# In every group VectorE adds the last quarter of the slots onto the third quarter, and TensorE's identity matmuls sum six of eight slots

## The chip, the cores and the metric

The kernel runs on one core of a Trainium2 chip. The metric is the device time of one execution in microseconds. TensorE (PE in the profile), VectorE (DVE), ScalarE (ACT), GpSimd (POOL) and SyncE (SP) are the five engines of the core. Each works through its own list of instructions in order, and they meet only at semaphores.

## What is computed

The reference is two layers over a graph of 6250 nodes and 200,000 edges, with 16 features each; the edges are sorted by their target node `dst`.

```python
w_m = (efeat @ W_msg + b_msg).reshape(E, in_f, -1)      # 16 x 16 per edge
w_a = (efeat @ W_attn + b_attn).reshape(E, in_f, -1)
h_src = feat[src][:, :, None]
e1 = w_m * h_src
e2 = w_a * h_src
ex = jnp.exp(e2 - seg_max[dst])
denom = segment_sum(ex, dst)
ft = segment_sum(e1 * (ex / denom[dst]), dst).sum(axis=1)
x = layernorm(x + ft)
x = layernorm(x + segment_mean(edge_attr, dst))
```

So each edge has 512 numbers of its own (256 of `e2`, 256 of `e1`), made from its 16 attributes and from the 16 features of its source node. For each node the sums over its edges of `ex` and of `e1 * ex` are wanted. 200,000 edges of 512 numbers are what the time goes into.

## The kernel before

Nodes are sorted by degree and put into 49 tiles (`NC`) of 128 nodes, one node per partition. Tile k has `DEG[k]` slots, from 56 down to 22: slot j holds the j-th edge of each of its 128 nodes. All 49 tiles have 1630 slots, of which 1607 need features. A tile's slots are cut into groups of 8 or 6 (`sizes`, `GRP`): 152 groups of 8 and 69 groups of 6, 221 in all.

For each slot, in order:

- GpSimd gathers the features of the 128 source nodes, with one indirect DMA per slot (`gather`, L647 to L653), into `HGF`, a ring of 80 slots (`FR`). Per tile it also loads the edge records (`edges_of`, L657), and for 36 tiles it scatters a result (L694). The index of each indirect DMA is a column in SBUF.
- TensorE transposes the edge attributes (`T`, L1097), ScalarE copies them out of PSUM (`evac`, L888), and TensorE makes the 512 weights of the slot (`W`, L1108) in one of two pairs of PSUM banks.
- VectorE multiplies two slots' weights with the gathered features into `EMR`, a ring of 64 slots (`mult`, L1472, a custom instruction that takes the maximum along). Before a tile's first multiplication `floors` (L1458) waits until the gathers of the tile have landed; only in the first and the last tile it waits group by group.
- Once a tile is complete its maximum is known. ScalarE takes the exponential of the first half of the group into PSUM (L944), then of the whole group in place (L946), then copies the second half's (L950) into PSUM. VectorE multiplies each half with its exponentials (`gm`, L1485).
- TensorE sums the slots of the group: one fp32 matmul with the identity per slot, all accumulated in the PSUM tile `PDR` (`gsum`, L1111 to L1131). After the last group of a tile ScalarE copies `PDR` out (L894) and VectorE divides and reduces (`weigh`, L1504 to L1506).

The order is written out by hand as `STEPS` (L106 to L118), 236 steps. In step i group p is produced (T, W, `mult`) and group c is consumed (exponentials, `gm`); TensorE sums the group that was consumed in step i-1. In TensorE's list the parts are interleaved (L1143 to L1149): up to four pairs of W, and behind each of them a quarter of the sums, that is 2 slots; T of group p+2 comes after the second quarter. On VectorE a step is two `mult`, `gm` of the first half, two `mult`, `gm` of the second half, and then what a new tile needs (L1600 to L1635).

For the last four groups alone (`ADDS`, L145) there is one operation more: `pairs` (L1487 to L1493) adds, in SBUF, the last slots of the second half onto the slots before them, and `gsum` leaves those last slots out. `KEPT(half)` is how many slots of the second half are kept: 2 of 4 in a group of 8, and 2 of 3 in a group of 6.

```python
def pairs(g):
    half = GRP[g][2] // 2
    keep = KEPT(half)
    v.wait_ge(S["a_exp"], g + 1)
    v.wait_ge(S["v_gm"], 2 * g + 2)
    sums = em(g, half, 2 * half - keep)
    v.tensor_tensor(sums, sums, em(g, half + keep, 2 * half), ALU.add).then_inc(S["v_ad"], 1)
```

Of the kernel before, what the change touches and what calls it, by code (L numbers as in the profile page):

```python
# [94 lines left out]
for g in range(NGR):  # L95
    n = GRP[g][2]
# [9 lines left out]
STEPS, MADE, USED, p, c = [], {}, {}, 0, 0  # L106
# [17 lines left out]
for g in range(NGR):  # L124
    k, n = GRP[g][0], GRP[g][2]
# [16 lines left out]
FINS = {USED[LAST[k]]: k for k in range(NC)}  # L142
NST = len(STEPS) + 4
NORMS = [p for p, c in STEPS].index(FIRST[MAIN + 4] + 2)
ADDS = [c for p, c in STEPS[-8:] if p is None]  # L145


def KEPT(n):
    return (n + 1) // 2


def gnn_kernel(nc, xt, dst, src, ea, eat, es, wc, cst, cst2, out):
# [14 lines left out]
    with ctx:  # L167
# [3 lines left out]
        def sem(name):  # L171
            return ctx.enter_context(nc.semaphore(name))
# [226 lines left out]
        S = {n: sem(n) for n in names}  # L399
# [42 lines left out]
        def em(g, lo=0, hi=None):  # L442
            hi = GRP[g][2] if hi is None else hi
            return EMR[:, 512 * (AT[g] + lo):512 * (AT[g] + hi)]
# [10 lines left out]
        def part(k, lo, hi):  # L455
            return XP[:, roff[k % 2]:roff[k % 2] + DEG[k], lo:hi]
# [588 lines left out]
        def _(pe):  # L1045
# [38 lines left out]
            def regular():  # L1084
                pe.wait_ge(S["v_xm"], 2)
                pe.wait_ge(S["g_m"], 9)
                pe.wait_ge(S["d_w2"], 160)
                pe.wait_ge(S["v_id"], 1)

                def T(g):  # L1090
                    k, j0, n, a = GRP[g]
                    pe.wait_ge(S["v_x3"], k + 1)
                    pe.wait_ge(S["a_p"], 4 * k + 4)
                    if g >= 1:
                        pe.wait_ge(S["a_T"], g)
                    for j in range(n):
                        i = pe.transpose(PTB[0:K, 128 * j:128 * j + 128], part(k, 0, K)[:, j0 + j, :], IDB[:, :])  # L1097
                    i.then_inc(S["p_T"], 1)

                def W(g, x):  # L1100
                    s = FROM[g] + x
                    if x == 0:
                        pe.wait_ge(S["a_T"], g + 1)
                    if s >= 2:
                        pe.wait_ge(S["v_mult"], s - 1)
                    for j in range(2):
                        lo = 128 * (PAIR[s][1] + j)
                        i = pe.matmul(PAIRS[s % 2][:, j, :], LT[:, g % 3, lo:lo + 128], WS[:, :], start=True, stop=True)  # L1108
                    i.then_inc(S["p_W"], 1)

                def gsum(g, lo, hi):  # L1111
                    k, j0, n, a = GRP[g]
                    half = n // 2
                    if g in ADDS:
                        n = half + KEPT(half)
                    for j in range(lo, min(hi, n)):
                        if j == 0:
                            if a == 0 and k >= 1:
                                pe.wait_ge(S["a_dn"], k)
                            pe.wait_ge(S["a_exp"], g + 1)  # L1120
                            pe.wait_ge(S["v_gm"], 2 * g + 1)
                        if j == half:
                            if g in ADDS:
                                pe.wait_ge(S["v_ad"], ADDS.index(g) + 1)
                            else:
                                pe.wait_ge(S["v_gm"], 2 * g + 2)
                        x = em(g, j, j + 1).rearrange("p (i a o) -> p a i o", a=2, o=16)
                        i = pe.matmul(PDR, IDN, x, start=(a == 0 and j == 0),  # L1128
                                      stop=(g == LAST[k] and j == n - 1))
                        if j == n - 1:  # L1130
                            i.then_inc(S["p_g"], 1)  # L1131

                T(0)
                T(1)
                W(0, 0)
                W(0, 1)
                for i in range(NST):
                    p, c = STEPS[i] if i < len(STEPS) else (None, None)
                    nx = STEPS[i + 1][0] if i + 1 < len(STEPS) else None
                    old = STEPS[i - 1][1] if 1 <= i <= len(STEPS) else None  # L1140
                    ahead = [(p, x) for x in range(2, GRP[p][2] // 2)] if p is not None else []
                    ahead += [(nx, 0), (nx, 1)] if nx is not None else []
                    for x in range(4):  # L1143
                        if x < len(ahead):
                            W(*ahead[x])
                        if old is not None:
                            gsum(old, 2 * x, 2 * x + 2)
                        if x == 1 and p is not None and p + 2 < NGR:
                            T(p + 2)  # L1149

# [109 lines left out]
        def _(v):  # L1260
# [154 lines left out]
            def regular():  # L1415
# [21 lines left out]
                def diff(k):  # L1437
                    v.wait_ge(S["v_ev"], k + 1)
                    if k >= 1:
                        v.wait_ge(S["a_p"], 4 * k)  # L1440
                    v.tensor_tensor(RM[:, 0:DEG[k], :], edge(k), upper(edge(k)), ALU.subtract).then_inc(S["v_x1"], 1)
# [19 lines left out]
                def mult(s):  # L1461
                    g, j = PAIR[s]
                    k = GRP[g][0]
                    if j == 0:
                        v.wait_ge(S["v_hm"], HMS[g])
                        if OLD[g] is not None:
                            v.wait_ge(S["p_g"], OLD[g] + 1)
                    v.wait_ge(S["p_W"], s + 1)
                    w = PAIRS[s % 2].rearrange("p j (i c) -> p (j i) c", c=32)
                    hb = feat(g, j, j + 2).unsqueeze(2).broadcast_to([128, 32, 32])  # L1470
                    x = s - FROM[FIRST[k]]
                    v.tensor_tensor_reduce(em(g, j, j + 2).rearrange("p (x c) -> p x c", c=32), w, hb, 1.0, LOW, ALU.mult, ALU.max,  # L1472
                                           accum_out=MXC[:, k % 2, x:x + 1]).then_inc(S["v_mult"], 1)
# [13 lines left out]
# [7 lines that stand above are left out]
# [102 lines left out]
                for i in range(NST):  # L1596
                    p, c = STEPS[i] if i < len(STEPS) else (None, None)
                    nx = STEPS[i + 1][0] if i + 1 < len(STEPS) else None
                    ahead = [FROM[p] + x for x in range(GRP[p][2] // 2)] if p is not None else []
                    for s in ahead[0:2]:  # L1600
                        mult(s)
                    if c is not None:
                        gm(c, 0)
                    for s in ahead[2:4]:
                        mult(s)
                    if p is not None and p == LAST[GRP[p][0]]:
                        collapse(GRP[p][0])
                    if c is not None:
                        gm(c, 1)
                        if c in ADDS:  # L1610
                            pairs(c)
                    if nx is not None:
                        k = GRP[nx][0]
                        if k in (0, NC - 1):
                            floors(nx, nx + 1)
                        elif nx == FIRST[k]:
                            for seg in SEGS:
                                if GRP[seg[0]][0] == k:
                                    floors(seg[0], seg[-1] + 1)
                    if p is not None:  # L1620
                        for k in range(1, NC):
                            if p == max(FIRST[k] - 6, 0):
                                valid(k)
                            if p == FIRST[k] - 5:
                                diff(k)
                            if p == FIRST[k] - 4:
                                low(k)
                            if p == FIRST[k] - 3:
                                mean(k)
                    if i - 3 in FINS:  # L1630
                        weigh(FINS[i - 3])
                        if FINS[i - 3] >= NC - 2:
                            joined(FINS[i - 3])
                    if 0 <= i - NORMS < 14:
                        main(i - NORMS)  # L1635
# [358 lines left out]
```

## Time and profile before

| | us |
|---|---|
| median of 3 runs without the profiler | 2243.48 (2243.09 to 2245.55) |
| span of the profiled execution, first to last instruction | 2950.2 |
| PE busy (matmuls) | 2137.9, 72% |
| DVE busy | 1862.0, 63% |
| POOL busy | 1687.5, 57% |
| ACT busy | 1256.9, 43% |
| granted TensorE clock, mean | 0.861 |

The profiled execution took 706.7 us longer than the median of the runs, so shares of its span can't be read as shares of 2243. Durations of single instructions can be read, and so can the time that one engine waited for another. PE is the busiest engine by the page.

### The profile page before, as it was taken

Reading aid. Unit: us, or ns where it says so; the run is one execution under the profiler, and the core shown is the slowest. Engines: PE = TensorE matmul, PEld = TensorE weight load, DVE = VectorE, ACT = ScalarE, POOL = GpSimd, SP = SyncE. Lnnn points to the kernel's source line nnn. Section 1 sums busy time; section 2 is a strip of 40 time slices with the busy share of each in tenths; the row PEclk is TensorE's granted clock in tenths of the full one; section 3 lists DMA queues with packets and bytes.
Section 4 is the critical chain, followed back from the end, with each engine's and each line's share of the span. In section 5 each row is a group of like instructions: output and inputs, shape, how many; then the busy total and the mean of one; then the engine's idle time right before and its main releaser. Section 6 shows DMA issues by size and latency. Waiting matters only on the chain. (4 is left out here: it accounts for less than half of the span.)

```text
span 2950.2 us, 21765 instructions
## 1 busy us (share of the span) xinstructions
PE 2137.9 (72%) x6682; PEld 952.6 (32%) x6682; DVE 1862.0 (63%) x2907; ACT 1256.9 (43%) x1228; POOL 1687.5 (57%) x1845
## 2 busy tenths in 40 slices
PE   2347676676877777877787658877787767887777
PEld 1213233232333333333333223333333323333333
DVE  6246465566666666666676547766667656786776
ACT  3223443434444443454454325444444444554444
POOL 6556355665655565555565465655656565655633
PEclk8658888897988888989888889988989888988988
DMA  6000000000000000000000000000000001001000
GB/s 229 16 10 11 8 12 10 10 10 9 10 9 9 14 10 9 10 14 10 10 13 9 9 10 13 10 12 9 10 12 9 12 9 28 12 8 16 8 2 3
DMA packets 60073, 47.60 MB, mean 16 GB/s; under 512 B 28366, under 2 KB 55439, under 8 KB 59436
## 3 DMA queue, kind: packets, MB, share of 16 engines
q0 software_dynamic: 57632, 29.73, 8.0%
q1 hardware_dynamic: 2316, 16.38, 1.5%
q8 instruction: 57, 0.93, 0.1%
q14 instruction: 68, 0.56, 0.1%
HBM read 44.00 MB, written 1.90 MB: 16 GB/s over the span
## 5 line engine op out<-in xcount | busy, mean ns | idle before, releaser
L652 POOL DMA_INDIRECT AR<-in_xt,AR x1607 | 1538.8, 958 | 974.1 <-DVE AR L1472 491.3
L1128 PE MATMUL PX<-AR,CS 128*128 128x512 f32 x3246 | 1663.7, 642 | 37.8 <-issue 23.9
L1472 DVE CUSTOM_DVE_ANT_1 AR<-PW,AR 128x1024 f32<-128x1024 f32 x815 | 979.6, 1221 | 896.8 <-remote 651.2
L1108 PE MATMUL PW<-WS,LT 100*128 100x512 bf16 x1630 | 549.1, 423 | 683.9 <-DVE AR L1472 511.8
L1128 PEld LDWEIGHTS PX<-AR,CS 128*128 128x128 f32 x3246 | 664.9, 206 | 652.1 <-issue 532.4
L888 ACT ACTIVATE LT<-PTB 100x1024 bf16<-100x1024 bf16 (+1 forms) x221 | 211.2, 956 | 1005.7 <-remote 601.0
L1485 DVE TENSOR_TENSOR AR<-AR,PX 128x1024 f32<-128x1024 f32 (+1 forms) x442 | 501.0, 1134 | 121.3 <-ACT PX L944 76.0
L1108 PEld LDWEIGHTS PW<-WS,LT 100*128 100x128 bf16 x1630 | 141.5, 103 | 1113.7 <-DVE AR L1472 543.2
L946 ACT ACTIVATE AR<-AR 128x2048 f32<-128x2048 f32 (+1 forms) x221 | 412.9, 1869 | 7.2
L950 ACT ACTIVATE PX<-AR 128x1024 f32<-128x1024 f32 (+1 forms) x221 | 212.4, 961 | 412.3 <-DVE AR L1485 294.8
L944 ACT ACTIVATE PX<-AR 128x1024 f32<-128x1024 f32 (+1 forms) x221 | 231.0, 1045 | 39.4 <-DVE AR L1485 30.1
L1097 PEld LDWEIGHTS PTB<-IDB,AR 128*100 128x100 bf16 x1630 | 133.4, 135 | 139.0 <-issue 138.2
L1097 PE MATMUL PTB<-IDB,AR 128*100 128x128 bf16 x1630 | 138.4, 231 | 10.3 <-ACT AR L922 9.1
L657 POOL DMA_INDIRECT AR<-in_es,E0I x48 | 47.1, 982 | 169.5 <-DVE AR L1472 143.4
L894 ACT ACTIVATE AR<-PX 128x512 f32<-128x512 f32 x49 | 29.2, 597 | 144.7 <-PE PX L1128 66.1
L1504 DVE RECIPROCAL AR<-AR 128x256 f32<-128x256 f32 x49 | 85.5, 1746 | 1.9 <-ACT AR L894 1.9
L1472 DVE DVE_READ_ACCUMULATOR2_ANT AR<- 128x1 f32 x815 | 67.6, 83 | 0.0
L914 ACT ACTIVATE AR<-AR 128x1024 bf16<-128x1024 bf16 (+13 forms) x49 | 54.8, 1119 | 0.0
L922 ACT ACTIVATE AR<-AR 128x1024 bf16<-128x1024 bf16 (+13 forms) x49 | 54.1, 1105 | 0.0
L1497 DVE TENSOR_REDUCE AR<-AR 128x16 f32<-128x512 f32 (+13 forms) x49 | 52.3, 1067 | 0.0
L694 POOL DMA_INDIRECT y_d<-AR x36 | 36.0, 1000 | 11.0 <-issue 11.0
L1458 DVE TENSOR_TENSOR AR<-AR 128x128 f32<-128x128 f32 (+14 forms) x71 | 36.7, 536 | 0.9 <-issue 0.2
(192 smaller groups left out, 517.7 us busy)
## 6 DMA issues: line engine op xcount, KB each, us to landing
AR<-in_xt,AR POOLq DMA_INDIRECT x1607
AR<-in_eat SPq DMA_DIRECT2D x3, 3128.0 KB
AR<-in_eat SPq DMA_DIRECT2D x1, 3120.0 KB
y_d<-AR SPq DMA_DIRECT2D x1, 784.0 KB
AR<-y_d SPq DMA_DIRECT2D x1, 784.0 KB
AR<-in_es,E0I POOLq DMA_INDIRECT x48
y_d<-AR POOLq DMA_INDIRECT x36
CS<-in_cst SPq DMA_DIRECT2D x1, 442.0 KB, 5.3
```

The source lines that it names most:

```text
L652: g.indirect_dma_start(feat(h, j - j0, j - j0 + 1), None, xt, bass.IndirectOffsetOnAxis(ap=node, axis=0)).then_inc(hg_sem(h), 16)
L888: a.activation(LT[:, g % 3, 0:128 * n], PTB[0:K, 0:128 * n], ACT.Copy).then_inc(S["a_T"], 1)
L914: a.activation(part(k, 0, 96).rearrange("p j (x w) -> p j x w", x=2)[:, :, :, 0:16], twice(h), ACT.Copy)\
L944: a.activation(half(w), x[:, 0:w, :], ACT.Exp, bias=shift).then_inc(S["a_x"], 1)
L946: a.activation(x, x, ACT.Exp, bias=shift).then_inc(S["a_exp"], 1)
L950: a.activation(half(w), x[:, w:2 * w, :], ACT.Copy).then_inc(S["a_x"], 1)
L1097: i = pe.transpose(PTB[0:K, 128 * j:128 * j + 128], part(k, 0, K)[:, j0 + j, :], IDB[:, :])
L1108: i = pe.matmul(PAIRS[s % 2][:, j, :], LT[:, g % 3, lo:lo + 128], WS[:, :], start=True, stop=True)
L1128: i = pe.matmul(PDR, IDN, x, start=(a == 0 and j == 0), stop=(g == LAST[k] and j == n - 1))
L1472: v.tensor_tensor_reduce(em(g, j, j + 2).rearrange("p (x c) -> p x c", c=32), w, hb, 1.0, LOW, ALU.mult, ALU.max, accum_out=MXC[:, k % 2, ...
L1485: v.tensor_tensor(y, y, EXP[:, 0:16 * w].rearrange("p (x o) -> p x o", o=16), ALU.mult).then_inc(S["v_gm"], 1)
L1504: link(v.reciprocal(RRT, d[:, 0:256]))
```

## The change

Every group is now treated as the last four were. `ADDS` is gone. VectorE calls `pairs` for each group right behind its second `gm`. `gsum` always sums `half + KEPT(half)` slots, 6 of 8 or 5 of 6, and its second half waits for the addition (`v_ad`) and no longer for `gm`. The sums behind the four pairs of W are no longer 2, 2, 2, 2 but 1, 2, 1, 2 slots (`GSUM`).

```diff
-ADDS = [c for p, c in STEPS[-8:] if p is None]
+
+
+GSUM = [(0, 1), (1, 3), (3, 4), (4, 6)]
...
                     half = n // 2
-                    if g in ADDS:
-                        n = half + KEPT(half)
+                    n = half + KEPT(half)
...
                         if j == half:
-                            if g in ADDS:
-                                pe.wait_ge(S["v_ad"], ADDS.index(g) + 1)
-                            else:
-                                pe.wait_ge(S["v_gm"], 2 * g + 2)
+                            pe.wait_ge(S["v_ad"], g + 1)
...
                         if old is not None:
-                            gsum(old, 2 * x, 2 * x + 2)
+                            gsum(old, *GSUM[x])
...
                     if c is not None:
                         gm(c, 1)
-                        if c in ADDS:
-                            pairs(c)
+                        pairs(c)
```

## Rows read from the trace of the kernel before

**Rows 1.** Groups by line and form: busy us, mean ns of one, idle before it

```profile
L1128 PE MATMUL PX<-AR,CS 128*128 128x512 f32 x3246 | 1663.7, 642 | 37.8 <-issue 23.9 <-ACT AR L894 13.8
L652 POOL DMA_INDIRECT AR<-in_xt,AR x1607 | 1538.8, 958 | 974.1 <-DVE AR L1472 491.3 <-issue 478.7 <-DMA AR<-in_es,E0I 3.1
L1472 DVE CUSTOM_DVE_ANT_1 AR<-PW,AR 128x1024 f32<-128x1024 f32 x815 | 979.6, 1221 | 896.8 <-remote 651.2 <-PE PW L1108 145.7 <-issue 83.4
...
L657 POOL DMA_INDIRECT AR<-in_es,E0I x48 | 47.1, 982 | 169.5 <-DVE AR L1472 143.4 <-DVE E0I L1398 18.1 <-issue 8.1
```

**Rows 2.** TensorE in order of time: start us, us, line, how many

```profile
107.33 1.06 PE L1097 MATMUL PTB<-IDB,AR 128*100 128x128 bf16 x8 [9.10 <-ACT AR L922]
...
2863.38 0.60 PE L1108 MATMUL PW<-WS,LT 100*128 100x512 bf16 x2
2863.81 1.88 PE L1128 MATMUL PX<-AR,CS 128*128 128x512 f32 x4
2865.53 0.61 PE L1097 MATMUL PTB<-IDB,AR 128*100 128x128 bf16 x8
2865.98 0.60 PE L1108 MATMUL PW<-WS,LT 100*128 100x512 bf16 x2
```

**Rows 3.** GpSimd in order of time: the start of tile 1, and the last gather

```profile
91.58 0.94 POOL L657 DMA_INDIRECT AR<-in_es,E0I  x1 [18.13 <-DVE E0I L1398]
95.64 0.94 POOL L652 DMA_INDIRECT AR<-in_xt,AR  x1 [3.12 <-DMA AR<-in_es,E0I]
96.89 0.94 POOL L652 DMA_INDIRECT AR<-in_xt,AR  x1 [0.30 <-issue]
...
2800.94 0.94 POOL L652 DMA_INDIRECT AR<-in_xt,AR  x1 [0.30 <-issue]
```

**Rows 4.** VectorE in order of time: the last `mult`, and additions of the last groups

```profile
2898.59 1.22 DVE L1472 CUSTOM_DVE_ANT_1 AR<-PW,AR 128x1024 f32<-128x1024 f32 x1
...
2906.11 1.22 DVE L1485 TENSOR_TENSOR AR<-AR,PX 128x1024 f32<-128x1024 f32 x1 [1.87 <-ACT PX L950]
2907.43 1.23 DVE L1493 TENSOR_TENSOR AR<-AR 128x1024 f32<-128x1024 f32 x1
2908.58 1.75 DVE L1504 RECIPROCAL AR<-AR 128x256 f32<-128x256 f32 x1
...
2926.15 0.69 DVE L1493 TENSOR_TENSOR AR<-AR 128x512 f32<-128x512 f32 x1
2926.76 1.74 DVE L1504 RECIPROCAL AR<-AR 128x256 f32<-128x256 f32 x1
```

**Rows 5.** VectorE and GpSimd: gathers that start inside an operation with two SBUF inputs

```profile
526.02 1.08 DVE L1448 TENSOR_TENSOR AR<-AR 128x896 bf16<-128x896 f32 x1
526.18 1.74 POOL L652 DMA_INDIRECT AR<-in_xt,AR  x1 [0.30 <-issue]
...
1777.95 0.69 DVE L1441 TENSOR_TENSOR AR<-AR 128x512 f32<-128x512 f32 x1
1778.03 1.42 POOL L652 DMA_INDIRECT AR<-in_xt,AR  x1 [0.30 <-issue]
```

**Rows 6.** The same where the VectorE operation reads one input from PSUM

```profile
1540.61 1.22 DVE L1472 CUSTOM_DVE_ANT_1 AR<-PW,AR 128x1024 f32<-128x1024 f32 x1
1541.14 0.94 POOL L652 DMA_INDIRECT AR<-in_xt,AR  x1 [0.30 <-issue]
1541.75 1.22 DVE L1485 TENSOR_TENSOR AR<-AR,PX 128x1024 f32<-128x1024 f32 x1
```

**Rows 7.** Single lines with two SBUF inputs: duration ns min/median/max (L1441), busy and mean (L1458)

```profile
L1441 DVE TENSOR_TENSOR AR<-AR x49: 517/690/1087, 104.0 to 2838.0; 128x512 f32<-128x512 f32 x7, 128x480 f32<-128x480 f32 x7, 128x544 f32<-128x544 f32 x6, 128x608 f32<-128x608 f32 x5
...
L1458 DVE TENSOR_TENSOR AR<-AR 128x128 f32<-128x128 f32 (+14 forms) x71 | 36.7, 536 | 0.9 <-issue 0.2
```

**Rows 8.** Two stretches: busy us of PE, PEld, DVE, ACT, POOL; granted clock

```profile
1498.00:1526.00 28.00, 27.65 (x93) 12.69 (x92) 23.16 (x34) 13.75 (x15) 14.24 (x16) 1.00 0.06 5
1538.00:1549.00 11.00, 7.92 (x19) 2.98 (x20) 10.17 (x16) 9.31 (x9) 8.26 (x10) 0.53 0.17 31
```

## The prediction

> **What bounds the kernel now.** I read the page first, then the groups by form, then each engine in order of time. By the page PE is the bound: 2137.9 us busy. But the profiled execution is 706.7 us longer than the median without the profiler, 2243.48, and the first thing to settle is where these went. 651.2 us of them are VectorE's: it stands before `mult` with a releaser that the trace does not name ("remote"), in 123 stalls [rows 1]. 2950.2 - 651.2 = 2299, near the median; I take these stalls to belong to the profiled execution. So I use its durations and ask what each engine would need without them.
>
> TensorE: in a stretch without stalls it is busy for 27.65 of 28 us at granted clock 1.00, its full level of 2.4 GHz [rows 8]. There a pair of W takes 0.43 us, four sum matmuls (two slots) 1.72 us, eight transposes 0.45 us [rows 2]. The 3246 sum matmuls [rows 1] are two for each of 1623 slots: 3246 x 0.43 = 1396 us. W is 815 x 0.43 = 350 us, the transposes 1630 / 8 x 0.45 = 92 us. Sum 1838 us. It begins at 107.3 [rows 2], and the end without work of its own is some 20 us: 1965 us, 278 less than measured.
>
> GpSimd: gathers follow each other every 1.25 us (95.64, 96.89), 0.94 us and 0.30 of issue, wherever it does not wait [rows 3]. Its idle time behind VectorE is 491.3 + 143.4 = 634.7 us [rows 1], nearly the stalls' 651.2: it waits for free slots of the ring only because VectorE stands. The last gather starts at 2800.9 [rows 3]; without those waits at 2166.2. To that: landing, 4.1 us by the edge record (issued at 91.58, its reader starts at 95.64) [rows 3]; `floors` and three `mult` of the last group, 3.7; and from the end of the last `mult` at 2899.8 [rows 4] to the end of the span, 50.4. Sum 2224 us, 19 below the median.
>
> So the GpSimd list of some 1690 indirect DMAs is the bound, not PE. It is a floor that the change doesn't lower: tile k can't start until its gathers have landed, and the next tile's are issued meanwhile. A tile of 38 slots costs GpSimd 38 x 1.25 and 2.5 for the record and the result, 50 us; TensorE 38 x (0.86 + 0.215 + 0.056) = 43 us.
>
> **What the change removes.** 149 groups of 8 and 68 of 6 are new in it (152 and 69 less the last four). TensorE loses 2 x 149 + 68 = 366 slots, 732 matmuls x 0.43 = 315 us. All of it lies beside GpSimd's list: worth nothing at the end. In the tail nothing goes either, the last four groups had it already. TensorE's total falls to 1523 us.
>
> **What it adds.** 217 operations on VectorE, just the form of L1493. One of 128x1024 starts 1.32 us after the `gm` before it and not 1.14, as it waits for that one's result, and the next operation follows 1.15 us later: 1.33 us in all. That of 128x512 is 0.61 + 0.18 = 0.79 [rows 4, 6]. 149 x 1.33 + 68 x 0.79 = 252 us. Does VectorE become the bound? Its list today: `mult` 815 x 1.15 = 937; `gm` 304 x 1.14 + 138 x 0.86 = 465; the page's other busy time 1862.0 - 979.6 - 67.6 (its accumulator reads) - 501.1 = 314. Sum 1716, then 1968; from 107 to its end some 2095 us, below GpSimd's 2224. Per tile of 38 slots: 40 us now, 46 then, against 50. So I cost this at nothing, but the cover is down to a tenth; if it were gone, each per cent more on VectorE's list would be 20 us.
>
> **The waits.** `pairs` waits for the group's exponentials, which the `gm` before it already had. Queued behind it are `floors`, the preparation of tiles and the next two `mult`; TensorE's W waits for those, with two pairs of PSUM banks between. TensorE's new wait for `v_ad` concerns the group of the step before, and stands behind a W that needs a later `mult`: never last. The split 1, 2, 1, 2 moves no W by more than 0.86 us; I cost it at zero, with GpSimd's list as the cover. DMAs are neither added nor moved in any queue.
>
> **What it costs GpSimd.** The addition has both inputs in SBUF, and there are four lines of this kind in each tile now (L1434, L1441, L1448, L1458). When a gather starts inside one, it is held. At 526.18 it starts 0.16 us into L1448 and takes 1.74 us, not 0.94; at 1778.03 it starts 0.08 into L1441 and takes 1.42 [rows 5]. Held time is in both the rest of the operation less 0.12 or 0.13 us. A gather that starts inside a `mult`, one input of which is in PSUM, takes 0.94 [rows 6]. So an addition of 1.23 us holds a gather by at most 1.10 us, one of 0.69 by 0.565. With a gather every 1.25 us at a phase that is not tied to VectorE's, the mean is 1.10² / 2.5 = 0.484 us, and 0.128. Sum: 149 x 0.484 + 68 x 0.128 = 81 us, all of it on the list that bounds. Bounds from both sides: no gather ever meets an addition, 0; each meets one at its start, 149 x 1.10 + 68 x 0.565 = 202. Check of the mean on today's lines: 147 of 0.69 us and 71 of 0.54 [rows 7] should hold by 147 x 0.128 + 71 x 0.07 = 24 us if GpSimd never waited; the gathers' mean of 958 against the usual 942 ns is 1607 x 0.016 = 26 us [rows 1]. So the mean is not too high, perhaps low. I take 85.
>
> The Trainium skill has both readings on one page, "SBUF — State Buffer", section "Who interferes with whom". It says that a VectorE instruction with two SBUF inputs contends with a GpSimd instruction that reads SBUF, and an indirect DMA reads its index column there; but it also infers that making descriptors needs only the write side, so that `tensor_tensor` does not stall such DMAs. By the second the time would stay at 2243. The trace agrees with the first: 0.80 us held.
>
> **Sum.** 2243.5 + 85 = 2328 us (+3.8%). Against the profiled execution's own sum: 2224 + 85 = 2309 and the 19 us that my floor lacks. Own range of this case: 2285 to 2350.
>
> **Rivals.**
> 1. Faster. The 1.25 us per gather may be a price of the profiler; without it GpSimd would be quicker and PE the bound of today. For it: PE is back to back in clean stretches [rows 8], and 1838 / 0.861, the profiled mean clock, + 127 = 2262 is near the median too. Against it: the half level (0.53) comes where PE has been idle [rows 8], and a PE that bounds has no such idle time. Then VectorE's 2095 plus some 50 of waits at 49 tile starts decides: 2145. It decides once GpSimd's floor and the 85 together are under 2243, that is at a real pace below 1.25 x (2158 - 154) / (2224 - 154) = 1.21 us (154 is what of the floor is not pace: 95.6 ahead and 58 behind).
> 2. No change. GpSimd bounds, but gathers and additions don't meet: the additions come at a fixed place of a step and might fall in step with the gathers, or GpSimd has slack that the profile hides. 2243. Against: rows 5.
> 3. Much slower. PE now has work for 1523 of 2330 us, 65%, in many short pieces, and may be granted the 1.2 GHz level more often. It decides once the mean clock is under 1523 / 2200 = 0.69; at 0.65 it is 1523 / 0.65 + 127 = 2470. In the stretch at 0.53 PE was busy for 7.92 of 11 us [rows 8]; but stretches as poor as that followed stalls.
>
> **Chances.** Forecast 0.66, rival 1 0.14, rival 2 0.10, rival 3 0.07, others 0.03. The range from 2240 to 2365 takes in rival 2 and more than the forecast's own range; outside are rival 1 and most of rival 3. A measurement of this kernel can tell about 0.2%, 4.5 us, from no change. Rival 2 goes mostly into "same", rival 1 and a bit of it into "faster": faster 0.16, same 0.08, slower 0.76.
>
> **What would show it.** In the profile after: 2514 sum matmuls; L1493 x221; L652's mean well above 958 ns, by 85 / 1.6 = 53 ns if GpSimd never waited, less as far as it waits; gathers of up to 2.0 us that start within L1493 and none within `mult`; GpSimd's idle time behind VectorE no smaller than its stalls make it. I am wrong on the bound if the time falls below 2230, wrong on the hold if L652 keeps its mean, and wrong on the clock if the granted mean without stalls is under 0.7.

## The result, and the profile after

| | before | after |
|---|---|---|
| median of the runs made together, us | 2243.28 (2241.71 to 2245.55, 4 runs) | 2310.03 (2307.34 to 2312.91, 4 runs) |
| ratio, 95% interval | 1 | 1.0296 (1.0282 to 1.0311) |

The change makes the kernel 66.8 us slower. The forecast was 2328, its range 2240 to 2365.

The profiled execution of the changed kernel took 2307.9 us, as long as its unprofiled runs; the stalls of 651.2 us [rows 1] are not in it. First the page's busy times, then the groups by line (busy us, mean ns of one, idle before it and what ended it). Numbers of lines have moved by two: L652 is now L654, L657 is L659, L1128 is L1126, L1472 is L1470, L1458 is L1456, L1493 is L1491.

```profile
span 2307.9 us, 20735 instructions
## 1 busy us (share of the span) xinstructions
PE 1762.1 (76%) x5950; PEld 792.0 (34%) x5950; DVE 2067.3 (90%) x3124; ACT 1257.8 (54%) x1228; POOL 1738.0 (75%) x1845
```

```profile
L654 POOL DMA_INDIRECT AR<-in_xt,AR x1607 | 1587.0, 988 | 493.2 <-issue 485.1 <-DVE AR L1470 3.7 <-DMA AR<-in_es,E0I 3.0
L1126 PE MATMUL PX<-AR,CS 128*128 128x512 f32 x2514 | 1311.3, 637 | 4.7 <-ACT AR L896 4.7
L1470 DVE CUSTOM_DVE_ANT_1 AR<-PW,AR 128x1024 f32<-128x1024 f32 x815 | 967.4, 1219 | 27.4 <-PE PW L1110 17.8 <-PE PX L1126 4.9 <-issue 3.1
L1110 PE MATMUL PW<-WS,LT 100*128 100x512 bf16 x1630 | 549.7, 423 | 464.0 <-DVE AR L1470 462.6
...
L1491 DVE TENSOR_TENSOR AR<-AR 128x1024 f32<-128x1024 f32 x152 | 186.5, 1227 | 16.2 <-DVE AR L1483 0.5
...
L1491 DVE TENSOR_TENSOR AR<-AR 128x512 f32<-128x512 f32 x69 | 47.9, 694 | 7.2
```

What was to be removed is gone: 2514 sum matmuls and not 3246. TensorE now stands 462.6 us before W, waiting for VectorE. What was added is there: 221 additions, 234.4 us. The gathers' idle time is nearly all small pieces of 0.3 us of issue, one before each; GpSimd waits for VectorE for 3.7 us in the whole run. So nothing holds it back, and still its 1607 gathers take 988 ns each. Compared with [rows 1], where it is 958, that is 48 us of longer gathers.

Where these are, two stretches of the timeline show (start us, us, engine and line; in brackets the idle time before).

```profile
316.57 0.94 POOL L654 DMA_INDIRECT AR<-in_xt,AR  x1 [0.30 <-issue]
...
317.76 1.23 DVE L1491 TENSOR_TENSOR AR<-AR 128x1024 f32<-128x1024 f32 x1
317.82 1.98 POOL L654 DMA_INDIRECT AR<-in_xt,AR  x1 [0.30 <-issue]
...
1519.55 1.23 DVE L1491 TENSOR_TENSOR AR<-AR 128x1024 f32<-128x1024 f32 x1
...
1520.34 1.26 POOL L654 DMA_INDIRECT AR<-in_xt,AR  x1 [0.30 <-issue]
```

The first gather starts 0.06 us into the addition and takes 1.98 us, 1.04 more than its 0.94. The second starts 0.79 us into one and takes 0.32 more. Both come to 1.10 or 1.11 us after the addition's start: a gather that starts within a 1.23 us addition is held until 0.12 us before the addition's end. That is the law the prediction read from two older lines [rows 5]. Added up over all indirect DMAs that start in L1491 (gathers, and a few of the edge records and scatters), the time over 942 ns is 60.4 us, in 148 of them.

The law has an exception at its very start. Of 157 indirect DMAs that start in an addition at least 0.13 us before its end, 152 obey it within 0.05 us. The other five start within 0.044 us of the addition's own start and are not held at all; there the addition takes longer. One of them:

```profile
410.79 1.28 DVE L1491 TENSOR_TENSOR AR<-AR 128x1024 f32<-128x1024 f32 x1
410.81 0.94 POOL L654 DMA_INDIRECT AR<-in_xt,AR  x1 [0.30 <-issue]
```

The three long additions among these five take 1.26 to 1.30 us, not 1.23.

### The profile page after: what moved, and what is told of

Its sections match the earlier page's. It is cut to its first block and busy times, and to the rows that moved or that the text cites. A ratio compares the mean times of both kernels' runs of the same rounds, so it can differ in the third digit from the quotient of the medians.

```text
span 2307.9 us, 20735 instructions
## 1 busy us (share of the span) xinstructions
PE 1762.1 (76%) x5950; PEld 792.0 (34%) x5950; DVE 2067.3 (90%) x3124; ACT 1257.8 (54%) x1228; POOL 1738.0 (75%) x1845
## 5 line engine op out<-in xcount | busy, mean ns | idle before, releaser
L654 POOL DMA_INDIRECT AR<-in_xt,AR x1607 | 1587.0, 988 | 493.2 <-issue 485.1
L1126 PE MATMUL PX<-AR,CS 128*128 128x512 f32 x2514 | 1311.3, 637 | 4.7 <-ACT AR L896 4.7
L1470 DVE CUSTOM_DVE_ANT_1 AR<-PW,AR 128x1024 f32<-128x1024 f32 x815 | 967.4, 1219 | 27.4 <-PE PW L1110 17.8
L1110 PE MATMUL PW<-WS,LT 100*128 100x512 bf16 x1630 | 549.7, 423 | 464.0 <-DVE AR L1470 462.6
L1126 PEld LDWEIGHTS PX<-AR,CS 128*128 128x128 f32 x2514 | 517.5, 206 | 407.3 <-issue 292.6
L1483 DVE TENSOR_TENSOR AR<-AR,PX 128x1024 f32<-128x1024 f32 (+1 forms) x442 | 500.8, 1133 | 45.8 <-ACT PX L946 23.2
L1491 DVE TENSOR_TENSOR AR<-AR 128x1024 f32<-128x1024 f32 (+1 forms) x221 | 234.4, 1061 | 23.4 <-DVE AR L1483 0.5
L1099 PEld LDWEIGHTS PTB<-IDB,AR 128*100 128x100 bf16 x1630 | 126.2, 129 | 131.7 <-issue 129.8
L1099 PE MATMUL PTB<-IDB,AR 128*100 128x128 bf16 x1630 | 131.5, 224 | 10.3 <-ACT AR L924 9.0
L1456 DVE TENSOR_TENSOR AR<-AR 128x128 f32<-128x128 f32 (+14 forms) x71 | 37.2, 543 | 93.0 <-DMA AR<-in_xt,AR 92.4
L1470 DVE DVE_READ_ACCUMULATOR2_ANT AR<- 128x1 f32 x815 | 67.4, 83 | 0.0
L896 ACT ACTIVATE AR<-PX 128x512 f32<-128x512 f32 x49 | 29.2, 596 | 58.7 <-PE PX L1126 58.5
L659 POOL DMA_INDIRECT AR<-in_es,E0I x48 | 46.7, 974 | 14.6 <-issue 13.1
```

Source lines behind the costliest of these rows:

```text
L654: g.indirect_dma_start(feat(h, j - j0, j - j0 + 1), None, xt, bass.IndirectOffsetOnAxis(ap=node, axis=0)).then_inc(hg_sem(h), 16)
L1126: i = pe.matmul(PDR, IDN, x, start=(a == 0 and j == 0), stop=(g == LAST[k] and j == n - 1))
L1483: v.tensor_tensor(y, y, EXP[:, 0:16 * w].rearrange("p (x o) -> p x o", o=16), ALU.mult).then_inc(S["v_gm"], 1)
```

## The experiments

**The kernel before once more.** No edit.

> The kernel before, profiled once more, to see whether its 651 us of stalls with an unnamed releaser belong to the kernel or to that one profiled execution. Theory (GpSimd's list of indirect DMAs bounds, the stalls belong to the profiled execution): time 2243; if this execution has fewer stalls, GpSimd runs on from tile 1 to the last gather with next to no wait for VectorE, the gathers' mean rises from 958 to some 960 to 965 ns (more of them meet the existing operations with two SBUF inputs), and PE is idle for 15 to 20% of the span. Rival (PE bounds the kernel before): PE has next to no idle time between its start and the end, and GpSimd waits for free slots for 100 us or more.

The 651.2 us of stalls did not come back: the profiled execution took 2243.2 us. TensorE is busy for 1963.1 us of it, so idle for 12% and not for the 15 to 20% expected, and the gathers' mean is 956 ns, a little under the 960 to 965; GpSimd's gathers wait for VectorE for 7.3 us, where the rival asked for 100. This is the trace with which the others are compared. Its rows: the gathers, `mult`, and in order of time the last gather, the 721st `mult` and the last `mult`.

```profile
L652 POOL DMA_INDIRECT AR<-in_xt,AR x1607 | 1536.1, 956 | 493.1 <-issue 481.1 <-DVE AR L1472 7.3 <-DMA AR<-in_es,E0I 3.1
L1472 DVE CUSTOM_DVE_ANT_1 AR<-PW,AR 128x1024 f32<-128x1024 f32 x815 | 974.8, 1220 | 162.9 <-PE PW L1108 113.5 <-issue 24.8 <-PE PX L1128 22.5
...
2162.24 0.94 POOL L652 DMA_INDIRECT AR<-in_xt,AR  x1 [0.30 <-issue]
...
1955.93 1.22 DVE L1472 CUSTOM_DVE_ANT_1 AR<-PW,AR 128x1024 f32<-128x1024 f32 x1
...
2191.59 1.22 DVE L1472 CUSTOM_DVE_ANT_1 AR<-PW,AR 128x1024 f32<-128x1024 f32 x1
```

The same three in the changed kernel:

```profile
2214.25 0.94 POOL L654 DMA_INDIRECT AR<-in_xt,AR  x1 [0.30 <-issue]
...
2002.67 1.22 DVE L1470 CUSTOM_DVE_ANT_1 AR<-PW,AR 128x1024 f32<-128x1024 f32 x1
...
2256.15 1.22 DVE L1470 CUSTOM_DVE_ANT_1 AR<-PW,AR 128x1024 f32<-128x1024 f32 x1
```

So the last gather starts 52.0 us later; the gathers and the other indirect DMAs of this stretch are held for 77.5 us after and 26.4 before, and the difference, 51.1, accounts for nearly all of that delay. The 721st `mult` is 46.7 us later, the last one 64.6. What follows the last `mult` is the same (51.6 and 51.8 us from its start). The question for the other runs: are the 47 to 52 us the held gathers, and what are the 18 us between the 721st `mult` and the last?

**The addition with one input.**

```diff
-                    v.tensor_tensor(sums, sums, em(g, half + keep, 2 * half), ALU.add).then_inc(S["v_ad"], 1)
+                    v.tensor_reduce(ADR[:, 0:1], em(g, half + keep, 2 * half), AX.X, ALU.max).then_inc(S["v_ad"], 1)
```

> The changed kernel, with the added operation replaced by a reduction (maximum) over the same 1024 or 512 numbers: one SBUF input in place of two, about the same time on VectorE. The fourth quarter's slots are then left out of the sums. Theory (the addition costs because it holds gathers): the time goes back to 2243 to 2255 and the gathers' mean to 958 to 965 ns. Rival (VectorE's list, 252 us longer, has become the bound or trails GpSimd at the end): the time stays at 2300 to 2312. In between, about 2275, if each has half.

2260.06 us (2259.3 to 2260.67), ratio 1.0069 (1.0052 to 1.0086). VectorE does as much as in the changed kernel (2062.5 us busy, 2067.3 there), and 50 of the 67 us are gone. The gathers' group, and one of them that starts 0.10 us into the reduction:

```profile
L655 POOL DMA_INDIRECT AR<-in_xt,AR x1607 | 1535.0, 955 | 493.2 <-issue 478.8 <-DVE AR L1471 10.4 <-DMA AR<-in_es,E0I 3.1
...
1422.51 1.22 DVE L1492 TENSOR_REDUCE ADR<-AR 128x1 f32<-128x1024 f32 x1
1422.61 0.94 POOL L655 DMA_INDIRECT AR<-in_xt,AR  x1 [0.30 <-issue]
...
2160.44 0.94 POOL L655 DMA_INDIRECT AR<-in_xt,AR  x1 [0.30 <-issue]
...
2206.51 1.22 DVE L1471 CUSTOM_DVE_ANT_1 AR<-PW,AR 128x1024 f32<-128x1024 f32 x1
```

134 indirect DMAs start at least 0.13 us before the end of a long reduction and take 944 ns in the mean; in the changed kernel 124 start so in a long addition and take 1381. The last gather is as early as before (2160.4), the last `mult` is not (2206.5, 14.9 late). So the hold doesn't come from VectorE being busy or from its reading as such. The reduction also writes one number per partition and not 1024, but writing isn't the cause either: in the changed kernel 264 indirect DMAs start as early within the long `gm` (L1483), which writes 1024 numbers to SBUF and reads one input from PSUM, and they take 945 ns in the mean. What is left is the second input in SBUF. At 2260 the time is above the 2243 to 2255 of my expectation: a second loss, some 15 us, is VectorE's own.

This run also shows how the indirect DMAs' starts lie against the added operation when nothing is held. Had the law held for them, they would have been held for 83 us, which is what the prediction took.

**The addition alone, all slots still summed.**

```diff
-GSUM = [(0, 1), (1, 3), (3, 4), (4, 6)]
+GSUM = [(0, 2), (2, 4), (4, 6), (6, 8)]
...
-                    n = half + KEPT(half)
```

> The changed kernel, but TensorE sums all 8 (or 6) slots again, 2, 2, 2, 2 behind the four W; the additions stay, so the fourth quarter is counted twice. Theory (TensorE's relief is worth nothing, it lies beside GpSimd's list): 2305 to 2320, as the change. Rival (TensorE is close to the bound, and the relief hides part of the additions' price): 2243 + 250 or so, 2400 to 2500.

2316.99 us (2314.2 to 2320.08), ratio 1.0323 (1.0305 to 1.034). The indirect DMAs are held for 73.8 us and the last gather starts at 2209.8. TensorE's 732 matmuls bring the changed kernel 7 us at most; and as the pieces of the sums differ too, the run further down has to say which of the two brings them.

**The relief alone: six of eight slots summed, no addition.**

```diff
+GSUM = [(0, 1), (1, 3), (3, 4), (4, 6)]
...
-                    if g in ADDS:
-                        n = half + KEPT(half)
+                    n = half + KEPT(half)
...
-                            gsum(old, 2 * x, 2 * x + 2)
+                            gsum(old, *GSUM[x])
```

> The kernel before, but TensorE sums only 6 of 8 and 5 of 6 slots in every group and VectorE adds nothing (but in the last four groups, as before); the slots left out are not counted. This is the change's relief alone, 315 us of TensorE. Theory (GpSimd's list bounds): 2235 to 2245, no change. Rival (TensorE bounds the kernel before): 1960 to 2150.

2249.05 us (2246.14 to 2250.28), ratio 1.0016 (1.0006 to 1.0026). TensorE's busy time falls from 1963.1 to 1741.9 us and no time is gained by it; the kernel is, if anything, 0.2% slower. `floors` shows where it went: it waits for gathers 37 times and 211.0 us, where it waited 21 times and 96.8 in the kernel before.

```profile
L1460 DVE TENSOR_TENSOR AR<-AR x71: 244/583/1091, 89.0 to 2187.2; 128x128 f32<-128x128 f32 x11, 128x480 f32<-128x480 f32 x9, 128x256 f32<-128x256 f32 x7, 128x512 f32<-128x512 f32 x6
its engine sat idle before it (us, times) until:
  DMA AR<-in_xt,AR: 211.0, 37
```

**The addition in two and in four pieces.** The same numbers are added, by two or by four instructions.

```diff
-                    v.tensor_tensor(sums, sums, em(g, half + keep, 2 * half), ALU.add).then_inc(S["v_ad"], 1)
+                    w = 512 * (half - keep) // 4
+                    more = em(g, half + keep, 2 * half)
+                    for x in range(4):
+                        i = v.tensor_tensor(sums[:, w * x:w * x + w], sums[:, w * x:w * x + w], more[:, w * x:w * x + w], ALU.add)
+                    i.then_inc(S["v_ad"], 1)
```

> The changed kernel, each addition cut into two of half the size, with the same result. Theory (a gather that starts inside an operation with two SBUF inputs is held for the rest of that operation less 0.125 us): held time of an addition goes with the square of its length. Two pieces of 0.69 us hold 2 x 0.565 x 0.565 / 2.5 = 0.26 us where one of 1.23 held 0.48; of the 51 us that the additions put on GpSimd's list some 25 stay. VectorE's list grows by 217 x 0.07 = 15 us. Time 2285 to 2295. Rival (the additions take bandwidth or slots from GpSimd in proportion to what they move): list and time as in the change, 2310, or 2315 to 2325 with the further instructions.

> The changed kernel, each addition cut into four. Theory: four pieces of about 0.35 us hold 4 x 0.225 x 0.225 / 2.5 = 0.08 us; of the 51 us some 8 stay on GpSimd's list. VectorE's list grows by some 40 us against the change, and it trails GpSimd further at the end: the 15 us of the kernel with one input become 20 to 40. Time 2265 to 2295. Rival (in proportion to the data): 2310 or more, up to 2350.

In two: 2293.94 us (2293.67 to 2296.58), ratio 1.0228 (1.0213 to 1.0244). In four: 2290.5 us (2289.09 to 2294.89), ratio 1.0214 (1.0198 to 1.0229). One line of each, by source line (duration ns min/median/max):

```profile
L654 POOL DMA_INDIRECT AR<-in_xt,AR x1607: 940/944/1687, 25.7 to 2195.6; - x179
```

```profile
L654 POOL DMA_INDIRECT AR<-in_xt,AR x1607: 940/945/1592, 24.9 to 2189.7; - x179
```

Worked out from the traces, all in us:

| | held in the addition | held in all | last gather starts | from there to the end |
|---|---|---|---|---|
| before | 0 | 26.4 | 2162.2 | 81.0 |
| one piece | 60.4 | 77.5 | 2214.3 | 93.7 |
| two pieces | 37.5 | 58.5 | 2195.6 | 96.3 |
| four pieces | 23.0 | 53.8 | 2189.7 | 98.9 |

A gather is held by the piece that it meets, not by the next one too, so shorter pieces hold it for less. Both times lie in their expected ranges, but less was saved than expected: I had expected some 25 and 8 us to stay of the change's 51, and 37.5 and 23.0 are held in the additions. In four, this is the length that I took for a piece, 0.35 us; the pieces of 128x256 take 0.42, and with that the expectation's own formula gives 23. What is held in the additions falls from 60.4 to 23.0, in all only from 77.5 to 53.8: the operations directly behind the addition hold more gathers again. One that has been held by the addition goes on just before its end and has gone before the next operation could catch it; this shielding is worth some 9 us in one piece (17.1 us held outside the addition, 26.4 in all before) and is gone in four (30.8). `low` (L1448 before, L1446 after), which follows directly behind the addition in 45 of 49 cases, shows it: it holds for 5.1 us in the kernel before, 1.0 behind one piece and 6.4 behind four.

**The scatters left out of the kernel before.** It asks whether GpSimd's list sets the time also without a profiler.

```diff
-                    g.indirect_dma_start(YD, bass.IndirectOffsetOnAxis(ap=NODE[:, k:k + 1], axis=0), OUTR[:, k, :], None)\
-                     .then_inc(S["d_y"], 16)
+                    if k == MAIN - 1:
+                        g.indirect_dma_start(YD, bass.IndirectOffsetOnAxis(ap=NODE[:, k:k + 1], axis=0), OUTR[:, k, :], None)\
+                         .then_inc(S["d_y"], 16)
```

> The kernel before, with 1 in place of 36 of the scatters of results on GpSimd's list (L694); the output lacks the other 35 tiles' results. Nothing else changes on any engine. Theory (GpSimd's list bounds the kernel before, and its 36 scatters cost 1.29 us each as any other entry of it): 2243 - 35 x 1.29 = 2198, at most 10 us more if VectorE then trails. Rival (TensorE or VectorE bounds): 2238 to 2245.

2199.85 us (2196.78 to 2201.58), ratio 0.9803 (0.9788 to 0.9818), with 35 indirect DMAs fewer: 43.5 us by the medians, 1.24 us for each. TensorE's and VectorE's work is untouched. The pace of 1.25 us [rows 3] is that of unprofiled runs, and it is what bounds.

**The old operations of the kernel before in pieces.** Lines L1434, L1441, L1448 and L1458 in three pieces, then in two. One of the four:

```diff
-                    v.tensor_tensor(RM[:, 0:DEG[k], :], edge(k), upper(edge(k)), ALU.subtract).then_inc(S["v_x1"], 1)
+                    for lo, hi in cut(DEG[k]):
+                        e = edge(k)[:, lo:hi, :]
+                        i = v.tensor_tensor(RM[:, lo:hi, :], e, upper(edge(k))[:, lo:hi, :], ALU.subtract)
+                    i.then_inc(S["v_x1"], 1)
```

> The kernel before without the change, but its four operations with two SBUF inputs per tile (L1434, L1441, L1448, L1458) are each cut into three along the slots, with the same result. Theory: what they hold on GpSimd's list, 26 us, falls to a third or less: three pieces of 0.28 us hold 3 x 0.155 x 0.155 / 2.5 = 0.03 us where one of 0.69 held 0.13. 18 to 22 us come off the list, VectorE's grows by 400 x 0.06 = 24 us, which has room. Time 2222 to 2232, faster than both kernels. Rival (held time goes with the data, or VectorE's growth counts): 2243 to 2260.

> The kernel before, with VectorE's long SBUF-to-SBUF operations on two inputs (those of lines L1434, L1441, L1448 and L1458) each cut in two pieces instead of the three of the run e8_before_pieces; nothing else differs and all is computed. Theory (a gather that starts within such an operation is held until the operation's end less 0.12 us, and what is saved is only that held time, against more instructions on VectorE): held time over 942 ns of the gathers' DMAs 18 to 22 us where the kernel before has 26, so 2236 to 2240 us, within 0.1% of the version in three. Rival (the gain of that version came from another thing, such as the order in which VectorE's pieces release work): in two pieces the time is that of the kernel before, 2243 us, or under 2232.

In three: 2236.96 us (2235.2 to 2238.89), ratio 0.997 (0.996 to 0.9981). In two: 2235.08 us (2233.24 to 2235.64), ratio 0.9963 (0.9948 to 0.9977). Held time falls from 26.4 to 18.0 and 15.6 us, the last gather starts at 2154.2 and 2151.5. Both beat the kernel before and the changed one; the intervals don't tell the two apart. The first gained less than its expectation (2222 to 2232): I had put all of the 26 us to these four lines, and in the kernel before only 17.2 are held in them. They fall to 9.7 in three pieces and to 7.7 in two. The second came out just below what was expected, in its time (2236 to 2240) and in its held time (18 to 22).

```profile
L653 POOL DMA_INDIRECT AR<-in_xt,AR x1607 | 1526.9, 950 | 493.3 <-issue 481.2 <-DVE AR L1485 7.3 <-DMA AR<-in_es,E0I 3.2
```

**The sums in even pieces.** The changed kernel, with the pieces behind the four pairs of W cut as before the change.

```diff
-GSUM = [(0, 1), (1, 3), (3, 4), (4, 6)]
+GSUM = [(0, 2), (2, 4), (4, 6), (6, 8)]
```

> The changed kernel with one edit: the list by which a group's plane weights are summed and multiplied on is cut 2, 2, 2, 2 of the slots instead of as in the changed kernel, so that VectorE's products and TensorE's sums come in even pieces. The addition is untouched. Theory (what is lost is gathers held within the addition, and VectorE ending late behind the last gather): nothing changes, 2308 to 2313 us, held time over 942 ns of the gathers' DMAs 73 to 82 us. Rival (the order in which a group's pieces come ready sets when the addition starts against the gathers): an edit of this place moves the additions' starts and with them the held time by more than 10 us, so under 2300 or over 2322 us.

2326.94 us (2323.46 to 2329.04), ratio 1.0367 (1.0351 to 1.0384): 17 us worse than the changed kernel. Neither side of the expectation is right. My theory said that nothing changes; the rival has the time, over 2322, but for a cause, more held time, which is the wrong one, since it fell from 77.5 to 69.6 us and the last gather starts at 2205.8, 8.4 us earlier. The loss is behind it: 121.1 us from there to the end, 93.7 in the changed kernel. VectorE waits for W:

```profile
L1470 DVE CUSTOM_DVE_ANT_1 AR<-PW,AR 128x1024 f32<-128x1024 f32 x815 | 969.8, 1218 | 93.4 <-PE PW L1110 89.3 <-PE PX L1126 2.8 <-issue 0.3
...
2276.90 1.22 DVE L1470 CUSTOM_DVE_ANT_1 AR<-PW,AR 128x1024 f32<-128x1024 f32 x1
```

89.3 us, where it is 17.8 in the changed kernel. And it no longer waits for gathers. The line of `floors` from 440 us to the end, in this kernel and then in the changed one:

```profile
L1456 DVE TENSOR_TENSOR AR<-AR x57: 250/586/785, 495.4 to 2273.2; 128x480 f32<-128x480 f32 x8, 128x128 f32<-128x128 f32 x7, 128x512 f32<-128x512 f32 x6, 128x256 f32<-128x256 f32 x6
its engine sat idle before it (us, times) until:
who waited for it (us, times):
```

```profile
L1456 DVE TENSOR_TENSOR AR<-AR x57: 251/586/798, 495.6 to 2250.5; 128x480 f32<-128x480 f32 x8, 128x128 f32<-128x128 f32 x7, 128x512 f32<-128x512 f32 x6, 128x256 f32<-128x256 f32 x6
its engine sat idle before it (us, times) until:
  DMA AR<-in_xt,AR: 50.9, 22
```

In the changed kernel VectorE meets GpSimd 22 times in this stretch and for the last time at 1949 us; with even pieces never after 440. There VectorE's list with its waits is the bound for most of the run. The kernel with the full sums is the same case: it has even pieces too, and `floors` waits for gathers 3 times in it, for 21.1 us. Compared with that one (2316.99), fewer matmuls with even pieces bring nothing (2326.94), so the 7 us of the changed kernel are not TensorE's relief by itself; the pieces 1, 2, 1, 2 are worth 17. Why even pieces with fewer sums are 10 us slower than even pieces with all of them isn't settled; the two differ in how long TensorE works behind the third and the fourth pair, and I did not follow it further.

**The addition not in the late groups, and in them alone.** In groups 185 to 216 of 221, which the changed kernel consumes from about 1966 us on.

```diff
+ADDS = [g for g in range(NGR) if g < 185 or g >= NGR - 4]
...
-                    n = half + KEPT(half)
+                    if g in ADDS:
+                        n = half + KEPT(half)
...
-                            gsum(old, *GSUM[x])
+                            gsum(old, *(GSUM[x] if old in ADDS else (2 * x, 2 * x + 2)))
...
-                        pairs(c)
+                        if c in ADDS:
+                            pairs(c)
```

> The changed kernel without the addition in groups 185 to 216 of 221 (14 of 8 slots, 18 of 6; they are consumed from about 1966 us on); there TensorE sums all slots again, 2 behind each pair of W. The last four groups keep theirs, as in the kernel before. All is computed. Theory (until about 1950 us VectorE is held to the gathers' pace and the loss is held gathers; from there to the end VectorE sets the time, and each late addition is paid at its full length): the late additions' held time, 6.5 us, and what the changed kernel loses behind that point, 13 to 18 us, are gone, and all before it stays: 2286 to 2294 us. Rival (the whole loss is held gathers): only the 6.5 us come back, 2303 us.

> The mirror image: the kernel before, with the addition from group 185 on only (32 groups more than before; TensorE sums 6 of 8 slots there, in pieces of 1, 2, 1, 2). All is computed. Theory (from about 1950 us on VectorE sets the end): +13 to +20 us on the kernel before, 2256 to 2263 us, nearly all of it behind the last gather, whose start moves by 5 to 8 us only. Rival (the whole loss is held gathers): 6.5 us, 2250 us.

Beside these two the kernel before took 2247.59 us, 4 more than beside the changed kernel. Not late: 2293.35 us (2286.76 to 2297.01), ratio 1.0197 (1.0181 to 1.0212), so 22 us back by the two ratios (0.0099 x 2243) and 17 by the medians; the theory, 6.5 us and 13 to 18, asked for 20 to 24. Late only (the second has `g >= 185`): 2265.34 us (2260.36 to 2268.17), ratio 1.0067 (1.0052 to 1.0081), 15 to 18 us lost, a median 2 us above the expected 2256 to 2263. The 721st and the last `mult` of each:

```profile
1997.62 1.22 DVE L1475 CUSTOM_DVE_ANT_1 AR<-PW,AR 128x1024 f32<-128x1024 f32 x1
...
2230.93 1.22 DVE L1475 CUSTOM_DVE_ANT_1 AR<-PW,AR 128x1024 f32<-128x1024 f32 x1
```

```profile
1962.36 1.22 DVE L1475 CUSTOM_DVE_ANT_1 AR<-PW,AR 128x1024 f32<-128x1024 f32 x1
...
2214.82 1.22 DVE L1475 CUSTOM_DVE_ANT_1 AR<-PW,AR 128x1024 f32<-128x1024 f32 x1
```

Between them lie 233.3 and 252.5 us; before it was 235.7, after 253.5. So the last stretch takes 17 to 20 us longer exactly where the late additions are, whatever comes earlier. 27 of the 32 late additions lie in it, four before the 721st `mult` and one behind the last. The rival (2303 and 2250) is out. One thing of the theory is not as expected: in the kernel with late additions alone the last gather starts at 2176.2, 13.9 us later than before, and not 5 to 8. Of that, 5.5 us are there by the 701st `mult` (1910.9 against 1905.4), and the first of the added additions starts at 1925.5 only: this much two executions differ by themselves. The other 8.4 are about what was expected.

## Why the prediction came out

**What bounds: right.** GpSimd's list is the bound before. TensorE alone relieved brings nothing, 35 indirect DMAs fewer bring 1.24 us each without a profiler, and the last gather, put at 2166.2 when the waits are taken out, starts at 2162.2 in the undisturbed trace. Taking the 651.2 us for that execution's own was right: no later profile has them. What my floor of 2224 lacked, 19 us, lies behind the last gather: 58 us by my sum, 81.0 in the trace. I had let VectorE follow the last gather by one group; its last `mult` starts 29.4 us after it. That was the trace of the second term of the loss, and I passed over it. TensorE was closer to the bound than my 1838 us of work at full clock: it was busy for 1963.1 at a mean granted clock of 0.951.

**What it removes: right, worth nothing.** 732 matmuls fewer; alone, 1.0016.

**What it costs GpSimd: the right mechanism, the term mis-sized.** I took 85 us, from a mean of 0.484 us for each long addition. Measured are 60.4 us in the additions, and 51.1 net of the shielding of the operations behind them, which I had not thought of. The law of a single hold was right (152 of 157 within 0.05 us); the phase was wrong. I took the gathers' starts as spread evenly. The number that meet a long addition is what that gives: of the 144 long ones in the stretch of gathers 20 meet none, 17 by an even spread. But the starts within them are not even. By tenths of a us from the addition's start:

```
0.0  0.1  0.2  0.3  0.4  0.5  0.6  0.7  0.8  0.9  1.0
  8    5    6    7   12    8   18   19    9   17   15
```

Nearly two thirds lie in the later half, where little is left to be held for. "Not tied to VectorE's phase" was the step that failed, and the holds themselves tie it. In the kernel with one input, where nothing is held, the law put on the starts as they are gives 83 us; put on the changed kernel's it gives 64. How a hold moves the next starts is argued, not shown: a held gather goes on at a time that the addition's end sets, and the next ones follow 1.25 us apart.

Of the 34 us between 85 and 51, 4 are my rounding up of 81, some 2 are five additions behind the last gather, 15 the phase, 3 the few that start with the addition and are not held, and 9 the shielding. The old lines should have warned me. The same mean gives 24 us for them, and I set the 26 us of the gathers' longer mean beside it, but in the undisturbed trace only 17.2 of its 26.4 are held in the four lines, where 15 of 76 indirect DMAs that start in one of them begin within 0.042 us of its start and are not held. The rest is other lines and a few ns on each gather. So the mean was too high, not "perhaps low".

**What it adds to VectorE: costed at nothing, cost 18 us.** The additions took 234.4 us busy and little more in starts, as counted. The cover was there up to 1949 us, the last time `floors` waited for a gather. It was not there behind that point, where a tile has 22 to 28 slots, and where VectorE never waited for gathers in the kernel before either: its last such wait is at 1941. From there on VectorE sets the end. Between the 721st and the last `mult` it has 27 additions more, 11 x 1.33 + 16 x 0.79 = 27 us by my prices, and they came out at 17 to 18. Most of the difference is time in which it waited before: in this stretch its waits for W fall from 9.3 to 1.8 us, those for ScalarE by 0.7. TensorE's relief isn't what hides it, since with all slots still summed the stretch takes 253.7 us, as long as in the changed kernel. The prediction weighed the cover for a tile of 38 slots, and as one number for the run; the sum had to be made for the last tiles by themselves.

**The pieces 1, 2, 1, 2: costed at zero, right for a wrong reason.** They move no bound as they stand, but the cover that I named, GpSimd's list, would not have been there. With 2, 2, 2, 2 kept, the change would have cost 84 us.

**The sum.** +46.7 us until the 721st `mult` (held gathers), +17.8 from there to the last, +0.2 behind: the spans' 64.7. I had 85 and 0. The forecast of 2328 was 18 us too high, by an overestimate of 34 us net (85 against 51) and a loss of 13 to 18 us that was left out. That the two have opposite signs is luck; the forecast was closer than its terms.

**The rivals.** The first (1.25 us is the profiler's price, PE bounds) falls with the scatters. The second (no meeting) falls with the timeline. The third fell too: the granted clock's mean is 0.899, 0.951 in the kernel before; the relief alone has the same clock (0.901) and the time of before.

**The rule for two inputs in SBUF.** With one SBUF input a gather takes 944 ns, with two it is held. The Trainium skill, "SBUF — State Buffer", section "Who interferes with whom", says that an instruction with two SBUF inputs contends with one of GpSimd that reads SBUF: by that rule, the traces agree. Its inference that `tensor_tensor` does not stall the making of descriptors does not hold for these indirect DMAs, whose index column lies in SBUF: 60.4 us in 148 of them. That it is the reading of this column which is held up, no run here shows.

## What to carry to other kernels

- Where GpSimd issues indirect DMAs one after the other and they set the pace, count each VectorE instruction with two SBUF inputs as a delay of that list, of up to its length, and not as VectorE's time. With one input in PSUM nothing was held (945 ns), and shorter instructions hold for less; here cutting the old ones in two made the kernel 0.4% faster.
- Idle time of an engine is a cover only where it lies. Make the sum for the last stretch by itself, and look for the last time that the engine waits for the one that bounds.

## What was not expected of the hardware

- A gather that has been held is past before the next instruction starts: an addition shields the operation behind it (17.1 us held outside the additions, 26.4 without them, 30.8 behind additions in four pieces).
- When the gather and the addition start within 0.044 us of each other, the gather is not held and the addition takes up to 0.07 us longer (five cases in the changed kernel). On the old lines of the kernel before 15 of 76 go unheld in this way.
- The profiled execution of the kernel before had 651.2 us of stalls that none of the later ones had. The page's busy shares were of no use for the bound; durations of single instructions were the same in both (`mult` 1221 and 1220 ns, a gather 0.94 us).
